# Routing and scattering tokens in four groups during alignment, with the shared expert between them

## The reference, cut to what matters

```python
logits = jnp.clip(x @ router_w.T + routing_bias, -50.0, 50.0)
probs = jax.nn.sigmoid(logits)                      # 7 experts
topk_probs, topk_idx = jax.lax.top_k(probs, 1)      # one expert per token
...
shared_out = _swiglu(x, sw1, sw2, sw3)              # an eighth expert, for every token
total_weight = clip(0.5 + topk_probs + 1e-8, 0.5, 2.0)
return 0.5 / total_weight * shared_out + switched / total_weight
```

## Time and profile before

| | us |
|---|---|
| median of 3 runs | 326.61 (326.35 to 327.68) |
| the profiled execution, its own time | 327.79 |
| its span in the trace | 326.5 |
| PE busy in the span | 235.0 |
| DVE, ACT, POOL busy | 192.1, 137.1, 153.5 |

### The profile page before, as it was taken

One profiled execution on the slowest core, in us unless ns is written; L12 is line 12 of the kernel. 1 busy time (PEld: TensorE's weight loads), 2 busy tenths in 40 slices (PEclk: granted clock), 3 DMA queues, 4 the chain that ended last, 5 costly groups with the idle time before them and its releaser, 6 DMA issues.

```text
span 326.5 us, 5092 instructions
## 1 busy us (share of the span) xinstructions
PE 235.0 (72%) x1294; PEld 173.9 (53%) x1294; DVE 192.1 (59%) x754; ACT 137.1 (42%) x372; POOL 153.5 (47%) x223
## 2 busy tenths in 40 slices
PE   0088788986000000688699999998899999999993
PEld 0044466876000000577646666666578778787872
DVE  0479999871199987798167733443345444444541
ACT  1457576654431111699542222221144444434341
POOL 7166777557000000155100477773047666676766
PEclk9999799999755555679879999999799999999998
DMA  7999301122196000000000232223213434343330
GB/s 207 309 337 395 113 19 33 32 66 65 33 220 91 0 1 0 2 2 0 2 0 6 62 99 88 89 83 89 74 22 49 62 51 66 52 58 52 61 41 4
DMA packets 38747, 24.77 MB, mean 76 GB/s; under 512 B 8272, under 2 KB 36048, under 8 KB 38608
## 3 DMA queue, kind: packets, MB, share of 16 engines
q1 hardware_dynamic: 25928, 17.29, 18.6%
q0 software_dynamic: 6496, 4.24, 8.7%
q10 hardware_dynamic: 6296, 2.93, 5.2%
HBM read 14.53 MB, written 10.16 MB: 76 GB/s over the span
## 4 chain that ended last, share of the span: by engine, by line
PE 25%; POOL 18%; issue 9%; ACT 5%; DVE 2%; POOLq 0%; ACTq 0%; DVEq 0%
POOL out L944 18%; PE bank L689 7%; PE bank L675 7%; PE bank L690 6%; ACT pay L623 3%; ACT mk L601 2%; PE bank L634 1%; PE bank L609 1%; PE bank L872 1%; PE bank L873 1%; POOL rstds L159 1%; DVE bn L150 1%; ACT xT L630 0%; PE bank L626 0%; DVE xr L613 0%
## 5 line engine op out<-in xcount | busy, mean ns | idle before, releaser
L944 POOL DMA_INDIRECT out<-cn,xs x38 | 58.6, 1541 | 42.7 <-DVE cn L937 38.0
L730 POOL DMA_INDIRECT routed<-pay,pos_i x32 | 31.4, 983 | 34.4 <-DVE loan L822 24.9
L159 POOL TENSOR_TENSOR rstds<-ve,half 128x4 f32<-128x4 f32 x24 | 27.7, 1153 | 35.7 <-DVE ve L157 30.9
L928 DVE TENSOR_TENSOR cn<-bank,cn 128x352 f32<-128x352 f32 x38 | 19.9, 525 | 38.6 <-PE bank L873 38.6
L912 ACT COPY h_ffn<-bank 128x256 f32<-128x256 f32 x38 | 14.2, 373 | 46.2 <-PE bank L896 46.2
L692 ACT ACTIVATE cn<-bank 128x512 f32<-128x512 f32 (+1 forms) x24 | 14.3, 596 | 44.7 <-DVE xr L721 22.8
L888 PE MATMUL bank<-w_sb,h_ffn 128*128 (+1 forms) x228 | 31.8, 275 | 1.4 <-ACT h_ffn L913 1.4
L888 PEld LDWEIGHTS bank<-w_sb,h_ffn 128*128 128x128 f32 (+1 forms) x228 | 28.6, 191 | 7.6 <-issue 7.0
L872 PE MATMUL bank<-w_sb,xsT 128*128 x76 | 29.9, 476 | 0.4 <-DVE xsT L919 0.4
L873 PE MATMUL bank<-w_sb,xsT 128*128 x76 | 29.3, 468 | 0.0
L697 DVE TENSOR_TENSOR h_ffn<-bank,cn 128x512 f32<-128x512 f32 (+1 forms) x24 | 16.5, 689 | 16.0 <-PE bank L690 15.9
(11 more groups left out here) (194 smaller groups left out, 532.7 us busy)
## 6 DMA issues: line engine op xcount, KB each, us to landing
w_sb<-in_w SPq DMA_DIRECT2D x8, 352.0 KB, 7.6
routed<-fill ACTq DMA_DIRECT2D x1, 2470.0 KB, 15.5
xs<-routed SPq DMA_DIRECT2D x38, 65.0 KB, 1.9
xr<-in_x SPq DMA_DIRECT2D x8, 256.0 KB, 5.6
cn<-in_ctx SPq DMA_DIRECT2D x8, 256.0 KB, 6.1
cT<-in_ctxT SPq DMA_DIRECT2D x8, 256.0 KB, 5.9
out<-xr SPq DMA_DIRECT2D x8, 256.0 KB, 2.4
w_sb<-in_w SPq DMA_DIRECT2D x8, 192.0 KB, 9.6
```

Of the source, the lines that this page charges most:

```text
L159: return pool_done(pool.tensor_tensor(rstds[:, k, s], ve[:, k, s], half[:, s], ALU.pow))
L730: pool.indirect_dma_start(routed, bass.IndirectOffsetOnAxis(ap=pos_i[:, n:n + 1], axis=0), pay[:, n, :], None, bounds_check=NS * P - 1).th ...
L928: dve.tensor_tensor(g[:, i, 0:HID], U[i][:, 0:HID], g[:, i, 0:HID], ALU.mult).then_inc(s_h, 1)
L944: pool.indirect_dma_start(out_rows, bass.IndirectOffsetOnAxis(ap=xs[:, s % XB, ROW - 1:ROW].bitcast(U32), axis=0), y[:, s % 4, :], None, b ...
```

## The change

The table `routed` gets 4096 rows for each expert, so that an expert's first row is a constant (`first_row`) and a token's row is known as soon as the tokens before it are counted. `TABLE` is 7 * 4096 + 6 * 128 = 29440 rows, against 4864, and the same `fill` transfer writes it, in the same place of the program. Routing is done for four groups of 8 tiles (`route(r)`), each with a scan that carries the count over from the last group (`picked[:, :, 0]`). The alignment loop now issues, turn by turn: the phases of the chunks (the oldest chunk first), a part of a route, up to three puts on POOL, a unit of the shared expert, a further part of the route, another unit. The shared expert's PSUM banks are a ring of three, its order is one generator (`shared`). ACT fetches the table for Silu, not Sigmoid, before the stage. The number of rows per expert, and with it `up_at`, `down_at` and the new `rows_at`, is worked out after the last unit. SP reads each tile's row from `rows_at` by registers.

```diff
 NS = (TOK - NE) // P + NE
...
+GT = 8
+NG = NT // GT
+TABLE = NE * TOK + (NS - NT) * P
...
-            m_fill = load(act, routed.rearrange("(k p) r -> p k r", p=P), fill[:, None, :].to_broadcast([P, NS, ROW]), "fill_out")
+            m_fill = load(act, routed.rearrange("(k p) r -> p k r", p=P), fill[:, None, :].to_broadcast([P, TABLE // P, ROW]), "fill_out")
...
-        fetch_table(ACT.Sigmoid)
+        fetch_table(ACT.Silu)
...
+        def route(r):
...
+            after(dve, old("logit", 2 * r + 1), m_rb, old("prob", r - 1))
+            chain(dve.tensor_tensor(lg[:, :, :], lgp, rb[:, None, :].to_broadcast([P, GT, NE]), ALU.add))
+            m = chain(dve.tensor_scalar(lg[:, :, :], lg[:, :, :], -50.0, 50.0, ALU.max, ALU.min))
+            after(act, m)
+            m_pr = mark("prob", r, act_done(act.activation(pr[:, :, :], lg[:, :, :], ACT.Sigmoid)))
+            yield
...             (twelve chained DVE operations: expert, scan, weights)
+            yield
+            after(pe, m_scan)
+            pe_done(pe.matmul(RANK, tri[:, :], picked[:, :, 1:], start=True, stop=False))
+            m_rank = mark("rank", r, pe_done(pe.matmul(RANK, ones[:, :], before_t[:, :, 0:GT], start=False, stop=True)))
+            yield
...             (four chained DVE operations: pos_i, carry)
+        def put_rows(count):
+
+            for n in range(putting["next"], min(putting["next"] + count, NT)):
+                if not old("pos", n // GT):
+                    break
+                after(pool, old("pos", n // GT), old("norm", n // CT), m_fill if n == 0 else None, m_id if n == 0 else None)
+                pool.indirect_dma_start(routed, ...
...
+        def shared():
+            last, m_y = None, None
+            for c in range(NC):
+                m_up = up(c, 0)
+                if c:
+                    m_h = multiply(c - 1, KC - 1, *last)
+                yield
+                last, m_up = m_up, up(c, 1)
+                multiply(c, 0, *last)
+                if c:
+                    m_y = down_all(c - 1, m_h)
+                yield
+                last, m_up = m_up, up(c, 2)
+                multiply(c, 1, *last)
+                if c:
+                    finish_x3(c - 1, m_y)
+                last = m_up
+                yield
+            m_h = multiply(NC - 1, KC - 1, *last)
+            finish_x3(NC - 1, down_all(NC - 1, m_h))
...
+        while turn < 2 * NG + 5:
+            turn += 1
             if started < NC:
                 under_way.append(aligned(started))
                 started += 1
-            under_way = [g for g in under_way[::-1] if next(g, "end") != "end"][::-1]
+            under_way = [gen for gen in under_way if next(gen, "end") != "end"]
+            if turn >= 6 and turn % 2 == 0:
+                router = route((turn - 6) // 2)
+            if router:
+                next(router)
+            put_rows(3 if turn <= NC + 2 else NT)
+            if turn >= 5:
+                next(expert)
+            if router and turn % 2:
+                next(router)
+            if turn >= 5:
+                next(expert)
+            if router and turn % 2:
+                next(router, None)
+        put_rows(NT)
+        while next(expert, "end") != "end":
+            pass
+
+        after(pe, old("pos", NG - 1))
+        m = pe_done(pe.matmul(TOTAL, ones[:, :], before_t[:, :, GT], start=True, stop=True))
         after(dve, m)
+        chain(dve.tensor_tensor(cnt[:, :], TOTAL, first_row[:, :], ALU.subtract))
...             (lt, te, ends, ekc, ekf, up_at, down_at as before, then:)
+        chain(dve.tensor_tensor(skc[:, :, :], ekc[:, :, :], te[0:1, None, 0:NE - 1].to_broadcast([1, NS, NE - 1]), ALU.mult))
+        chain(dve.tensor_reduce(started_at[:, :], skc[:, :, :], AX_X, ALU.add))
+        chain(dve.tensor_tensor(started_at[:, :], iota_f[0:1, 0:NS], started_at[:, :], ALU.subtract))
+        chain(dve.scalar_tensor_tensor(started_at[:, :], ekf[:, :], float(TOK // P), started_at[:, :], ALU.mult, ALU.add))
+        m_rows = chain(dve.tensor_scalar(rows_at[:, 0:NS], started_at[:, :], float(P), None, ALU.mult))
...
             sp.wait_ge(s_put, NT * 16)
+            after(sp, m_rows)
             for s in range(NS):
+                if s % 4 == 0:
+                    sp.load(row_reg, rows_at[0:1, s:s + 4])
...
-                sp.dma_start(xs[:, s % XB, :], routed[s * P:(s + 1) * P, :]).then_inc(s_xi[s % XB], 16)
+                base = sp.snap(row_reg[s % 4], min_val=0, max_val=TABLE - P)
+                sp.dma_start(xs[:, s % XB, :], routed[bass.ds(base, P), :]).then_inc(s_xi[s % XB], 16)
```

More of the change, by code:

```diff
@@ L662, in program, with chain, over_e @@
[L662 to L669, removed]
+        def chain(ins):
+            m = dve_done(ins)
+            after(dve, m)
+            return m
+        def over_e(a):
+            return a[:, :, None].to_broadcast([P, GT, NE])
@@ L676, in down, with up @@
             return ins
-        def shared(c):
-            b = c % 2
+        def up(c, k):
+            j, kw = c * KC + k, KW[k]
             xc = xT[:, c * CW:(c + 1) * CW]
[L682 to L711, removed]
@@ new lines, in up @@
+            a, u = (2 * j) % 3, (2 * j + 1) % 3
+            wa = slice(k * P, k * P + kw)
+            wu = slice(HID + k * P, HID + k * P + kw)
+            after(pe, m_w13[SH], free.get(("ring", a)))
+            m_a = pe_done(pe.matmul(RING[a][0:kw, :], w13_sb[:, SH, wa], xc, start=True, stop=True))
+            after(pe, free.get(("ring", u)))
+            m_u = pe_done(pe.matmul(RING[u][0:kw, :], w13_sb[:, SH, wu], xc, start=True, stop=True))
+            after(act, m_a, free.get(("g", j % 2)))
@@ new lines, in up, with multiply @@
+            m_g = free[("ring", a)] = act_done(act.activation(g[0:kw, j % 2, :], RING[a][0:kw, :], ACT.Silu))
+            return m_u, m_g
+        def multiply(c, k, m_u, m_g):
+            j, kw = c * KC + k, KW[k]
+            u = (2 * j + 1) % 3
+            after(dve, m_g, m_u, free.get(("h", c % 2)) if k == 0 else None)
+            m = dve_done(dve.tensor_tensor(h[0:kw, c % 2, k, :], RING[u][0:kw, :], g[0:kw, j % 2, :], ALU.mult))
+            free[("ring", u)] = free[("g", j % 2)] = m
+            return m
@@ L712, in shared, with down_all @@
+        def down_all(c, m_h):
+            after(pe, m_h, m_w2[SH], old("x3", c - 1))
             for t in range(CT):
                 r = slice(t * P, (t + 1) * P)
[L714 to L718, removed]
+                m = pe_done(down(Y[:, t * D:(t + 1) * D], [(h[0:KW[k], c % 2, k, r], w2_sb[0:KW[k], SH, k, :]) for k in range(KC)]))
+            free[("h", c % 2)] = m
+            return m
@@ L736, in store_x3 @@
             sp.dma_start(rows(out)[:, c * CT:(c + 1) * CT, :], xr[:, c * CT:(c + 1) * CT, :]).then_inc(s_x3, 16)
[L738 to L778, removed]
@@ new lines, in program @@
+        under_way, started, turn = [], 0, 0
+        expert = shared()
+        router = None
+        while turn < 2 * NG + 5:
+            turn += 1
+            if started < NC:
+                under_way.append(aligned(started))
+                started += 1
+            under_way = [gen for gen in under_way if next(gen, "end") != "end"]
[12 more added lines that the diff above has]
+                next(router, None)
@@ L820, in program @@
+        chain(dve.tensor_tensor_scan(ends[:, :], onesf[:, 0:NE], te[:, :], 0.0, ALU.mult, ALU.add))
         chain(dve.tensor_tensor(ekc[:, :, :], ends[0:1, None, 0:NE - 1].to_broadcast([1, NS, NE - 1]),
@@ L861, in pe_tiles @@
             pe.load(up_reg, up_at[0:1, 0:4])
-            after(pe, *(free[("Y", b)] for b in range(2)))
             for s in range(2):
```

164 lines of the change are left out of this document (88 added, 76 removed).

## The result

The changed kernel takes 340.49 us (median of 4 runs, 340.31 to 341.26) against 327.14 us for the kernel before, run beside it. The ratio is 1.0414, 95% interval 1.0381 to 1.0447: slower. I had forecast 338.5, in a range of 330 to 347.

What follows compares the result with a forecast made beforehand. PE was taken to bound the kernel, so only its alignment idle time could be won. The last shared matmul 5.4 us later plus the tail's 6.5 gave 11.9, so 338.5 us, range 330 to 347.

Steps and rivals of the forecast that it cites:

- The start: First alignment matmul to first shared one: 15.5 us, with 6.9 of work and 8.6 idle or slow (bounds 5.5 and 10).
- Half clock behind it: First shared matmuls after the start: 1.0 us added because PE runs them at half clock.
- The gaps in the turns: Later turns: PE waits 1.2 us a turn for xT copy and normalising, 6.3 with late masks (bounds 3 and 11).
- 86.5 of work: PE's full-clock work from first alignment to last shared matmul: alignment 22.6, shared expert 62.6, rank matmuls 1.3 us.
- the last 0.85: End of the shared expert: the last `down` still waits 0.85 us for Silu and multiply.
- The tail: Last x3 to first tile transposes: counts, register reads and load take 7.75 us against 1.2, 6.5 later (5.5 to 8.5).
- The fill costs nothing: Filling `routed`: the six times longer fill lands near 176 and costs nothing while it lands before 181.
- The first rival: The fill blocks POOL and through it the alignment; landing at 199 gives 18 us more, 356; chance 0.12.
- a sign against it: Interleaved stage: the prediction is wrong if ACT shows more than one table load after 129.
- The second rival: Routes on ACT: Sigmoid and Silu switches cost two table loads per route, 4 us on the end, 342; chance 0.10.
- The other side: Interleaved stage without PE gaps: faster only if idle and slow time is under 4.0 us, not 15.9; chance 0.12.

Runs made afterwards that it cites:

- experiment 1: Changed kernel with the phases of a turn reordered so DVE makes the next chunk's masks before the last chunk's x2 and statistics: 335.54 us.
- experiment 4: Changed kernel with the totals' matmul and the thirteen DVE operations issued among the last six shared-expert units, not after them: 331.42 us.
- experiment 2: Changed kernel with the router's Sigmoid computed by Tanh, plus one small DVE operation per route: 339.79 us.
- experiment 6: Changed kernel with masks before x2, and transposes and xT copy moved between the turn's two shared-expert units: 334.27 us.
- experiment 9: Changed kernel with the split turn, Tanh for Sigmoid, counts among the last units, and the one large fill kept on ACT: 319.44 us.
- experiment 12: Changed kernel with only the fill changed: small, in seven transfers from SP, started after ACT's last square root: 339.83 us.
- experiment 10: Changed kernel with the split turn, Tanh for Sigmoid, counts among the last units, and a small fill on SP after ACT's last square root: 319.70 us.
- experiment 11: The kernel of experiment 10 with the router's Sigmoid again in place of Tanh: 322.96 us.
- the split turn: Edit to the changed kernel's turn: masks before x2, transposes and xT copy between the two shared-expert units; alone 334.27 us.
- experiment 3: Changed kernel with the fill cut to 84 blocks of 128 rows, in seven transfers on ACT in place of one: 350.84 us.
- experiment 5: Changed kernel with the small fill of seven transfers issued by SP in place of ACT: 343.08 us.

## Why the prediction was right

**PE's work stays, and its idle time with it.** The stretch from the first alignment matmul to the last shared one is 103.0 us (131.24 to 234.2); I had 103.3. Its parts moved against each other:

- The start: forecast 15.5 us to the first shared matmul, measured 16.95. I had taken the alignment's matmuls at 1.14; with PE idle for much of each turn they ran at half clock, 2.08 each, which is 0.94 more in each of three turns. The order of masks and x2 on DVE was the right cause: experiment 1 turned it round and won 5.0 us, 4.3 of them in the start itself.
- Half clock behind it: forecast 1.0. The first unit takes 2.9 (148.19 to 151.10) in place of 1.72: 1.2.
- The gaps in the turns: forecast 6.3. Behind the first shared matmul the list of PE's waits has 2.4 for pay, 1.2 for xT, 1.0 for masks and 0.5 for Silu, 5.1 in all. What is left of 103.0 after 86.5 of work, 10.1 idle or slow at the start (16.95 less 6.9), 1.2 and the last 0.85 is 4.3, so the work was some 0.8 less than I had added up. A full turn has 0.46 (from 152.82, when the unit's last matmuls are through, to 153.28) and 0.5 for the two waits, not 0.55 and 0.65. The 0.5 for Silu stood behind a table load, which I had not counted here.

The start came out 1.5 longer than forecast, the gaps 1.2 shorter and the work 0.8 less; that the sum is off by only 0.3 is luck.

**The tail: forecast 6.5, measured 6.6.** From the last x3 to the first transposes are now 7.9 us (234.25 to 242.11), against 1.2. The thirteen operations took 3.93 (forecast 4.0), SP's read of the registers and issue 0.85 (239.23 to 240.08; forecast 0.6), the load 2.0 (1.9). The read is on the chain that ended last:

```profile
239.34 0.50 SPq L881
```

The Trainium skill, DMA: Bandwidth & Descriptors, section Latency and other measured facts, gives a tensor load a floor of about 0.6 us. This trace does not agree: its first such read takes 0.50 us, and the ten of SP have a median of 0.30. The issue behind the read makes up the rest of the 0.85. Experiment 4 removed the tail and 1.7 us more in the first tiles. I had not seen that PE starts the tiles at the lower clock, in the kernel before as well; against that kernel it is worth only the 0.3 between transposes and first scatter.

**The fill costs nothing.** Landing was forecast near 176 and came at 176.9 (88.4 plus 88.5). That it came so close is luck: the same fill in experiments 1, 2, 4, 6 and 9 took 77.5 to 80.0 us from issue to landing, which is near 167, and why it took longer in this execution is open. The first put did wait for it: it starts at 177.99, where POOL was free from 174.3, and at 175.35 in experiment 12 with the small fill. But POOL had made rstds and shift for chunk 6 by 183.4, and the normalising, at 186.62, came behind ACT's copy and not behind POOL. Experiments 9, 10 and 12 show it. The first rival did not come about.

**The tables.** Here the account of the forecast itself was wrong. I had named more than one table load after 129 as a sign against it, and there were eight. The second rival, to which I had given 0.10, had the mechanism right, four pairs of loads, but not the price of 4 us: 0.7 in the changed kernel, which is not told from nothing. I had priced it as if nothing else could be late at those places. The forecast, which had no term for them, was near by luck. The Trainium skill, ScalarE: Activation LUTs, section Table sets, says to group by set; the loads here are 1.283 us each, and following the rule pays 3.3 us only once the other waits are gone (experiment 11).

**The other side.** I had said that the new order could be faster only with under 4 us of idle time and slow clock, given its tail. Experiment 9 is faster than before, 0.978, because it takes away both: its tail is hidden, and its shared expert's last `down` starts at 217.58 in place of 231.27 (at 221.64 in ten, whose median is the same; the profile of nine is of its fastest execution). Eleven, with the table loads left in, is still faster than before, at 0.9885. The fault of the changed kernel lay in the order within a turn and in what was left behind the last unit, not in the idea of routing in groups.

The sum, on the spans: alignment and shared expert 5.1 longer, first transposes 6.6 later behind them, 0.6 in the tiles, 0.3 between transposes and first scatter, and 0.5 less before the alignment: 12.1. The last is no effect of the change: with the same program ahead of it, the first alignment matmul starts between 131.12 and 131.87 in experiments 1, 2, 4, 6 and 9. The medians differ by 13.35, not 12.1: the profiled execution before was 0.65 above its median and the one after 0.2 below, and the time outside the span is 0.4 longer. Against the median of the changed kernel the forecast was 2.0 us short.

## What to carry to other kernels

Interleaving two stages wins only the idle time of the engine that bounds both; add up its work, then walk one turn through each in-order queue and see which waits come back. Look at what is moved behind the last unit of the bounding engine: a chain of small operations that was free under it costs its full length there, and here 1.7 us of slower matmuls on top (experiment 4). A cost that is covered (the table loads) shows its price only when the waits around it are gone, so test it again after each gain; the split turn, worth 1.3 and then 5.9 us, is the same case.

## What the runs showed of the hardware that I had not expected

- A queue of ACT or SP holds its issuer from about the third large transfer in a row: 0.41, 0.83, 3.01 and then 16.79 us for four more on ACT, each of 780 KB (experiment 3), and 22.57 us for the seven on SP (experiment 5). One transfer of 14950 KB took 0.41 us to issue.
- A fill that starts beside small transfers, issued before it, makes them late by 2.8 us (experiment 5), though it holds no computing engine.
- PE's granted clock stayed at its lower level from 131 to 147 us, in which PE was busy for 10.45 of 16 us: 2.08 us for eight alignment matmuls in three turns running.
- PE's clock at a hand-over can fall behind a short pause: 1.27 us in the kernel before, with its first two tile matmuls at 1.50 us, against 0.85 behind a pause of 0.73 (experiment 4). What decides between them is open.
- Where the clock rises differs between executions of the same instructions (experiments 6 and 9: 1.91 and 1.02 us for the first two shared matmuls).
